# Causal scores from two rounded parts in partition halves, with stacks loaded through GpSimd's queue

## The reference, cut to what matters

```python
q, k, v = proj(wq, bq), proj(wk, bk), proj(wv, bv)      # of the layer norm of x; 16 heads of 16
scores = jnp.einsum('bhqd,bhkd->bhqk', q, k) * scale
attn = jax.nn.softmax(scores + mask, axis=-1)           # mask: the keys after the query
out = jnp.einsum('bhqk,bhkd->bhqd', attn, v)
```

## Time and profile before

| what | us |
|---|---|
| median of 3 runs | 2358.67 (2347.09 to 2362.86) |
| the profiled execution | 2356.39, of it the span 2354.7 |
| `prepare` | 0 to about 195 |
| first scoring of group 0 | about 195 to 223 |
| `causal_attention` in all | about 195 to 768 |
| one group in the steady state | 32.86 |
| all that follows | about 768 to 2354.7 |
| busy over the span | TensorE 2015.3, VectorE 1448.2, ScalarE 1241.8, GpSimd 798.6 |

### The profile page before, as it was taken

One profiled execution on the slowest core, in us unless ns is written; L12 is line 12 of the kernel. 1 busy time (PEld: TensorE's weight loads), 2 busy tenths in 40 slices (PEclk: granted clock), 3 DMA queues, 4 the chain that ended last, 5 costly groups with the idle time before them and its releaser, 6 DMA issues.

```text
span 2354.7 us, 36114 instructions
## 1 busy us (share of the span) xinstructions
PE 2015.3 (86%) x11968; PEld 1253.7 (53%) x11968; DVE 1448.2 (62%) x3942; ACT 1241.8 (53%) x2980; POOL 798.6 (34%) x663
## 2 busy tenths in 40 slices
PE   5566899999988736989989989989989989989988
PEld 3232233333322525666666666656767667657666
DVE  5467677787774435646646746646745745746744
ACT  1121566666667224745754754753754754754663
POOL 2233221112232335505505505614613613613620
PEclk9796899999999868999999999999999999999999
DMA  5646744554530541000000000011100000000000
GB/s 145 153 132 134 141 98 66 82 82 69 103 109 10 158 138 77 1 28 10 1 23 14 1 23 14 1 66 64 49 19 19 19 19 18 19 4 33 19 1 27
DMA packets 124455, 128.97 MB, mean 55 GB/s; under 512 B 50460, under 2 KB 101232, under 8 KB 123248
## 3 DMA queue, kind: packets, MB, share of 16 engines
q1 hardware_dynamic: 123696, 117.75, 21.6%
q0 software_dynamic: 576, 8.91, 1.0%
HBM read 75.51 MB, written 50.86 MB: 54 GB/s over the span
## 4 chain that ended last, share of the span: by engine, by line
PE 35%; DVE 13%; ACT 8%; issue 6%; POOL 2%; DMA 0%; DVEq 0%; SPq 0%; POOLq 0%; ACTq 0%
DVE rot_s L1862 5%; PE qkv_ps L1372 5%; PE s_ps L1412 4%; PE qkv_ps L1313 4%; PE s_ps L1359 3%; PE pt_ps L1425 3%; PE s_ps L1493 3%; PE o_ps L1450 3%; DVE p_sb L1871 3%; ACT p_sb L1605 2%; POOL inv_norm L1756 2%; PE pt_ps L1412 2%; PE o_ps L1412 2%; PE pt_ps L1493 2%; PE o_ps L1493 2%
## 5 line engine op out<-in xcount | busy, mean ns | idle before, releaser
L699 ACT ACTIVATE probs<-st_ps 128x512 f32<-128x512 f32 (+3 forms) x768 | 327.9, 495 | 185.9 <-PE st_ps L614 184.4
L1313 PE MATMUL qkv_ps<-w_qkv,x_parts 128*128 128x512 f32 x1152 | 309.2, 412 | 33.4 <-DVE x_parts L1836 24.1
L744 DVE CUSTOM_DVE_ANT_0 seen<-s_ps,causal 128x128 f32<-128x128 f32 (+3 forms) x512 | 234.8, 485 | 90.1 <-PE s_ps L599 89.9
L1605 ACT ACTIVATE p_sb<-p_sb,negmax 128x256 f32<-128x256 f32 (+1 forms) x512 | 249.5, 490 | 71.4 <-DVE negmax L1871 71.1
L599 PE MATMUL s_ps<-k_stack,q_stack 96*128 96x512 bf16 (+3 forms) x768 | 244.7, 348 | 42.0 <-DVE piece_negmax L744 20.5
L1313 PEld LDWEIGHTS qkv_ps<-w_qkv,x_parts 128*128 128x128 f32 x1152 | 212.0, 194 | 81.2 <-issue 39.5
L614 PE MATMUL st_ps<-q_stack,k_stack 98*128 98x512 bf16 (+3 forms) x768 | 235.1, 337 | 19.0 <-ACT probs L699 14.4
L1871 DVE CUSTOM_DVE_ANT_0 p_sb<-s_ps,band 128x256 f32<-128x256 f32 (+1 forms) x512 | 185.5, 401 | 89.9 <-PE s_ps L1359 85.2
L1621 ACT COPY p_t<-pt_ps 128x512 f32<-128x512 f32 (+1 forms) x256 | 143.6, 561 | 162.5 <-PE pt_ps L1425 161.1
L821 POOL TENSOR_SCALAR_AFFINE_SELECT probs<-probs 128x512 f32<-128x512 f32 x128 | 81.6, 637 | 433.0 <-ACT probs L699 433.0
L1764 POOL TENSOR_TENSOR rot_c<-qn,turn_by 128x512 f32<-128x512 f32 x128 | 178.6, 1415 | 137.8 <-PE turn_ps L1339 111.9
(11 more groups left out here) (146 smaller groups left out, 3505.1 us busy)
## 6 DMA issues: line engine op xcount, KB each, us to landing
qk_scratch<-parts SPq DMA_DIRECT2D x64, 192.0 KB, 2.8
q_stack<-qk_scratch SPq DMA_DIRECT2D x96, 128.0 KB, 6.7
k_stack<-qk_scratch SPq DMA_DIRECT2D x96, 128.0 KB, 7.1
w_ffn<-ffn_weights POOLq DMA_DIRECT2D x4, 2176.0 KB, 11.7
v_scratch<-v_out SPq DMA_DIRECT2D x32, 256.0 KB, 2.6
v_sb<-v_scratch SPq DMA_DIRECT2D x16, 512.0 KB, 10.0
x_in<-xt_scratch SPq DMA_DIRECT2D x16, 512.0 KB, 4.1
ffn_weights<-w_high SPq DMA_DIRECT2D x2, 2176.0 KB, 7.6
```

The costliest lines, as they stand in the source:

```text
L699: act.activation(probs[:, n % 3, h, q0:CH], st_ps[i % 3][:, q0:CH], ACT.Exp).then_inc(exp_done.sem, 1)
L744: dve.tensor_tensor_reduce(seen[:, i % 3, 0:kw], s_ps[i % 3][:, 0:kw], causal[:, CH - kw:CH], -1.0, BIG, ALU.add, ALU.min, result).then_in ...
L1313: mm = pe.matmul(qkv_ps[:, part * CH:(part + 1) * CH], x_parts[:, w % XR, xp, k, :], w_qkv[:, wp, k, part * INNER:(part + 1) * INNER], sta ...
L1605: act.activation(p_sb[:, u % 4, h, k0:PW], p_sb[:, u % 4, h, k0:PW], ACT.Exp, scale=-1.0, bias=negmax[:, u % 4, h:h + 1], accum_out=total[ ...
```

## The change

q and k are cut into two parts, both rounded to fp32r instead of bf16: the high one by VectorE, the low one by GpSimd as `full` minus high. `mid_low`, `rest` and their semaphores go. Three products (`TERMS`) give 48 rows; heads 0 and 2 lie in partitions 0 to 47, heads 1 and 3 in 64 to 111, and each matmul takes rows of one half. A stack has the same bytes. `load_stack` is issued by GpSimd (12 DMAs), for group 0 after the low part of step 4 in batch 1, for group 1 at the start of the causal stage, for groups 2 and 3 in `first` ahead of its masks, later after the bias of each group. v is loaded by SP on its own semaphore (`load_values`). The spreads move to GpSimd too, ahead of the masks of sets 8 and 10. Pieces are issued only after odd shifted scores, in pairs: the same piece of the two heads of a half. The rows of ones are set by GpSimd at the start of `prepare`. With the new order the shifts are turned at i = 24 and 40.

```diff
-TERMS = ((0, 0), (0, 1), (0, 2), (1, 0), (1, 1), (2, 0))
+TERMS = ((0, 0), (0, 1), (1, 0))
+ROWS = P // 2
-def load_stack(sp, a, stacks, g):
+def load_stack(pool, a, stacks, g):
-            sp.dma_start(stack[r * HD1:(r + 1) * HD1, slot, :, :],
-                         a["qk_scratch"][which, g, part].rearrange("(h d) t -> d h t", d=HD1))\
-                .then_inc(stack_in[slot], 16)
-    sp.dma_start(v_sb[:, slot], a["v_scratch"][g]).then_inc(stack_in[slot], 16)
+            for side in range(2):
+                pool.dma_start(stack[side * ROWS + r * HD1:side * ROWS + (r + 1) * HD1, slot, :, :],
+                               a["qk_parts"][which, g, part].rearrange("(j b d) t -> b d j t", b=2, d=HD1)[side])\
+                    .then_inc(stack_in[slot], 16)
+def load_values(sp, a, stacks, g):
+    sp.dma_start(v_sb[:, g % SLOTS], a["v_scratch"][g]).then_inc(values_in[g % SLOTS], 16)
...
-        parts = sb("parts", [P, 4, 3, CH], BF16)
+        parts = sb("parts", [P, 4, 2, CH], F32R)
...
-            def mid_low(b, i):
-                dve.wait_ge(rest_ready.sem, rest_ready.of(b, i))
-                dve.tensor_copy(parts[:, i % 4, 1, :], rest[:, i % 4, :]).then_inc(mid_ready.sem, 1)
-                dve.wait_ge(mid_ready.sem, mid_ready.of(b, i))
-                dve.tensor_tensor(parts[:, i % 4, 2, :], rest[:, i % 4, :], parts[:, i % 4, 1, :],
-                                  ALU.subtract).then_inc(low_ready.sem, 1)
...
+            for side in range(2):
+                if side:
+                    pool.wait_ge(ones_drawn, 1)
+                pool.memset(as_float(stacks[1][side * ROWS + ROWS // 2:(side + 1) * ROWS]), 1.0).then_inc(ones_drawn, 1)
...
-                    pool.tensor_tensor(rest[:, i % 4, :], full[:, i % 4, :], parts[:, i % 4, 0, :],
-                                       ALU.subtract).then_inc(rest_ready.sem, 1)
+                    pool.tensor_tensor(parts[:, i % 4, 1, :], full[:, i % 4, :], as_float(parts[:, i % 4, 0, :]),
+                                       ALU.subtract).then_inc(low_ready.sem, 1)
+                    if b == 1 and i == TC:
+                        for s in parts_stored:
+                            pool.wait_ge(s, 32 * (NI // 4 + 1))
+                        load_stack(pool, a, stacks, 0)
...
-        while i < NP * HG and taken < upto:
-            taken += PIECES[i % NP][2]
+        while at % 2 and i < NP * HG and (i % 2 or taken < upto):
+            taken += PIECES[i % (NP * HALF) // HALF][2]
...
-                pe.matmul(s_ps[i % 3][:, 0:kw], q_stack[0:STK, slot, h, qt * P:(qt + 1) * P],
-                          k_stack[0:STK, slot, h, k0:k0 + kw], start=True, stop=True).then_inc(s_ready.sem, 1)
+                pe.matmul(s_ps[i % 3][:, 0:kw], q_stack[rows, slot, h // 2, qt * P:(qt + 1) * P],
+                          k_stack[rows, slot, h // 2, k0:k0 + kw], start=True, stop=True).then_inc(s_ready.sem, 1)
...
+            def first(group):
+                spread_shift(group, 0)
+                spread_shift(group, 1)
+                for g in range(2, SLOTS):
+                    load_stack(pool, a, stacks, g)
+                pool.wait_ge(bias_in, 16)
             def group_work(group, previous, following):
                 for n in DIAGONAL:
+                    if following and n == DIAGONAL[TC]:
+                        spread_shift(following, 0)
+                    if following and n == DIAGONAL[TC + 2]:
+                        spread_shift(following, 1)
...
+                        upcoming = group[0] * SLOTS + group[1] - 1 + SLOTS
+                        if SLOTS <= upcoming < B * NG:
+                            load(upcoming)
```

## The result

The changed kernel takes 2614.51 us (median of 4 runs, 2609.31 to 2620.3) against 2359.96 for the one before (4 runs beside it, 2347.09 to 2362.86): a ratio of 1.109, 95% interval 1.104 to 1.114. It is 11% slower, 254.6 us, where 2330 was forecast and 2382 was the upper end.

A forecast was written before the change was run, and what follows sets the result against it. TensorE was taken to set the causal stage's pace, VectorE next; VectorE, then SP's stores, to set `prepare`. 2356.4 - 38.4 - 8 + 3.5 + 12 + 4 = 2329.5, so 2330 us, range 2280 to 2382.

The forecast's parts named there:

- TensorE's 22 us of a period: Causal stage: pairs in halves take some 8 us from TensorE's 30.4 per period, leaving 22.
- Rival E: Causal stage: gaps on TensorE lower the granted clock to 0.8, 5 us more per period, half covered; 2368, chance 0.07.
- the 33.1 of the period: Causal stage, per group: VectorE 26.0 plus 3.3 starved plus 3.8 at the seam, against 32.86 before; +4 us in all.
- the seam: Causal stage, between two groups: VectorE's wait for pieces would be 3.8 us against 3.2 before.
- its small gaps: Causal stage, VectorE starved within a period outside the seam by the new order of pieces: 3.3 us in all.
- 34.5 as the upper bound of a period: Causal stage: period if each fp32r weight load (194 ns against 99) shows behind every wait at a gap.
- -38.4, -8 and +3.5: `prepare`: 4.8 us saved in 8 chunks, 8 from moving stack 0's loads to GpSimd, 3.5 lost to its starting memset.
- Stack 0's chunk: `prepare`, around stack 0's loads: 8 us extra instead of 16.0, so 8 saved (0 to 13).
- The chunk itself: `prepare`, an ordinary chunk of 512 tokens: 14.2 us, or 15.0 at a granted clock of 0.92, instead of 19.8.
- Rival D: `prepare` gets no shorter since stores take VectorE's place: 38.4 + 8 back, 2376, chance 0.1.
- Rival C: Causal stage: GpSimd's queue becomes the wait, at 1.5 us per DMA masks come late; 2391, chance 0.18.
- The first mask: Start of causal stage: waits behind GpSimd's spreads and stack loads, 28 x 0.67 = 18.8 us; +12 us, once.

The follow-up runs named there:

- b_rows48: Kernel before with three of its six products, so 48 and 50 rows, in bf16, old order, one head at a time: 2602.58 us.
- b_rows64: Kernel before with four of its six products, so 64 and 66 rows, in bf16 and the old order: 2669.99 us.
- a_rows64: Changed kernel with its halves filled to 62 and 64 rows, q's added rows zeros and k's ones: 2524.61 us.
- a_full_old: Changed kernel, still fp32r, with score matmuls over all 128 rows (summing two heads) and the old order of pieces: 2395.04 us.
- b_order: Kernel before with only the change's new order of pieces, bf16 and 96 rows kept: 2407.71 us.
- a_bf16_full_old: Changed kernel with bf16 parts and stacks, score matmuls over all 128 rows (summing two heads) and the old order: 2349.33 us.
- b_vout4: Kernel before with four output buffers for v instead of two, a semaphore for each: 2329.38 us, ratio 0.987.
- a_bf16: Changed kernel with parts and stacks in bf16 instead of fp32r; halves, order and GpSimd's queue kept: 2512.46 us.
- b_fill96: Kernel before with three of six products, rows 48 to 95 zero but streamed, so 96 and 98 rows: 2393.72 us.

## Why the prediction was wrong, step by step

**The clock: the step that failed.** The sum took TensorE's 22 us of a period at the full clock, from halves side by side, and then asked only whether VectorE would starve. Rival E had the right direction (its sign in the profile, a clock under 0.95 in this stage, came) and three wrong sizes: chance 0.07, a clock of 0.8 where 0.53 was measured, and half covered. At 0.53 its own 22 us are 41.5, over the 33.1 of the period, so nothing is covered. (The 22 was low too: the 49.11 us measured at 0.53 are some 26 at the full clock, an estimate from that row.) It also looked for the cause in gaps: "with gaps on TensorE the granted clock leaves 1.00". There were no more than before: TensorE was busy for 49.11 of 51.38 us (30.39 of 32.86 in the earlier trace rows), and for 52.38 of 52.65 in `b_rows48`. The cause is the rows. Packing is not needed for it (`b_rows48` and `b_rows64` have one head at a time), and it doesn't make it worse: halves of 62 and 64 rows stood at 0.56 to 0.91, 64 and 66 rows unpacked at 0.50 to 0.63, though in another type and order. No row of before showed matmuls with few rows in bf16 or fp32r over a long stretch. The earlier trace rows had 64 rows in full fp32, in another stage with other work around it, and I took it as proof of packing. The clock around it would not have warned me: from 1140 to 1200 it is 0.97, with 9.1 of TensorE's 53.7 busy us in matmuls of 64 rows. The Trainium skill, TensorE: Matmul & The Clock Gate, section What's actually happening, says that the gate is set by how busy TensorE has recently been; in these runs a TensorE busy for 57.64 of 57.86 us is at 0.52 with 64 rows, and one busy for 30.38 of 32.86 us is at 1.00 with 80.

**The size of it.** Of the 18.5 us that the period gained, 0.8 are GpSimd's queue and the rest that no run takes apart (33.61), up to 1.3 with the dips (34.1), 1.5 fp32r (35.7), 2.3 the new order (38.0), each measured at a clock near 1.00; the last step, from full rows to halves, is 38.0 to 51.4, 13.4 us, and holds the clock's loss less what packing gives back. Over 15 periods that is 200 of the 265 us. What packing gives at the full clock is seen in stretches of `a_rows64`, here 3.5 us at 1.00:

```profile
605.15:608.66 3.51, 2.89 (x26) 1.61 (x23) 3.46 (x9) 2.72 (x6) 3.51 (x7) 1.00 0.77 222
```

```profile
605.15 0.51 PE L610 MATMUL st_ps<-q_stack,k_stack 64*128 64x512 f32 x2
605.49 0.35 PE L594 MATMUL s_ps<-k_stack,q_stack 62*128 62x384 f32 x2
...
607.75 0.46 PE L594 MATMUL s_ps<-k_stack,q_stack 62*128 62x512 f32 x2
607.99 0.39 PE L610 MATMUL st_ps<-q_stack,k_stack 64*128 64x512 f32 x1
```

A pair of pieces of 512 columns takes 0.24 us, as forecast (0.25), a pair of shifted scores 0.34, against 0.47 for two fp32r matmuls one after the other (`a_full_old`). A steady period of `a_rows64` is at best 38.92 us at 0.91, no shorter than the 38.0 of full rows at 1.00. What a whole packed period at 1.00 would take stays open.

**The order.** I had 33.1 for VectorE starved by bursts. `b_order` measures 35.65 with everything else as before: the mechanism held, the size was 2.5 us short, 38 us over 15 periods. 3.8 was right for the seam. VectorE is busy for 26.48 us instead of 26.00, and its small gaps come to 5.4 (35.65 - 26.48 - 3.8) where I had 3.3. Before's own period already has 3.7 of them (32.86 - 26.00 - 3.2, among them 1.8 for the transposes ahead of the two normalisations), so 3.3 for an order with bursts was too little on its face. The waits of `b_order`:

```profile
ACT probs L706 <- PE st_ps L621: 13.4, 14, 1.9
DVE seen L752 <- PE s_ps L606: 7.2, 6, 3.8
```

**The type.** Priced at nothing in the sum, 34.5 as the upper bound of a period. In `a_full_old` fp32r costs 1.5 us a period, with weight loads of 188 ns instead of some 100 in `a_bf16_full_old`, and neighbouring matmuls of 512 columns 0.24 us apart instead of 0.22; no run separates the two. With that alone in it (15 x 1.5 = 23) the sum would have been 2352, not 2330.

**`prepare`.** Of -38.4, -8 and +3.5 (42.9 earlier at the end), 18.1 came. The memset was right (`deviations` at 17.43 instead of 13.14, +4.3). The three ordinary chunks from 102.15 to 157.84 take 18.6 us each. Stack 0's chunk was better than forecast: from 59.80 to 102.15 it is two such chunks and 5.2 us more, where before had 16.0 more, so 10.8 came instead of 8. The chunk itself failed: 18.6 us, not 15.0 (and 14.2 us at a clock of 0.92 would have been 15.4 at most, not 15.0). I called VectorE the bound and added its wait for the v store to its work; `b_vout4` shows that the wait was the bound, in before, with VectorE's work left as it is. In the changed kernel that wait is 51.1 us from 26 to 170, more than before's 46.1, since the part stores in SP's queue carry 256 KB. Its bf16 twin `a_bf16`, with 128 KB, had 40.9 us and 16.6 us a chunk over all seven, where the changed kernel had 18.8. Rival D gave 19 us between v stores as its sign, and that came: the stores did take VectorE's place, and with them went half of the 46.4 us that D puts back (22.4 came between the first and the last v stores).

**GpSimd's queue.** A DMA costs 0.49 us (24 between 205.26 and 217.04), not 0.67, and the twelve of a group take 6 us of room that is over 14 wide. Rival C is out. The first mask waited for these loads, as forecast, and came 11.0 us earlier, not 30, mostly for what `prepare` did not give: behind the last v stores 7.1 us were lost, where 12 were forecast.

## What to carry to other kernels

Before matmuls are made smaller in rows to pack or to save bytes, look for a stage of the same kernel in which most matmuls have as few rows and read its granted clock; a few of them among others (the stage of the earlier trace rows, at 0.97) say nothing. If there is none, test the row count alone first, which in `b_rows64` was one line. Where a stage falls to the low clock with TensorE busy all the time, streaming rows of zeros beside the data can bring it back at no cost per period; the memsets cost time where an engine waits for them (35 us in `b_fill96`). And where an engine waits for the landing of its own store, try more buffers before taking work off it: two more and their semaphores brought 1.3% here.

## What the runs showed of the hardware

- In the causal stage the granted clock goes with the rows that the score matmuls stream. With the same 206 matmuls a period: 48/50 rows 0.50 to 0.66, 64/66 rows 0.50 to 0.63, 80/82 rows 1.00, 96/98 rows 1.00, and 1.00 with 48 of the 96 rows zero. It is a finding for this mix, in which values and transposes use all 128 rows.
- Rows are not all of it: in before's first scoring, with 96 rows and nothing beside it, TensorE is busy for 15.2 of the 20 us from 200 to 220, at 0.50.
- In the packed kernel, halves of 62 and 64 rows had 0.56 to 0.91 and those of 48 and 50 0.50 to 0.64. No run says why single periods swing.
- A GpSimd DMA of 128 KB into 16 partitions is issued in 0.49 us, and 24 in a row take 11.8 us.
- GpSimd's memset goes by elements of a partition, not by bytes or partitions: 16384 in bf16 took 13.75 us on two partitions and 13.8 on 32 (two in 27.55, `b_fill96`), 8192 in fp32 on 32 partitions 6.9 (two in 13.89, the changed kernel).
